# A scan's input term in a PSUM bank of its own, five shared banks in place of six, and a new order of the work

## The reference, cut to what matters

```python
def step(h, inp):
    dtt, ut, bt, ct = inp
    dA = dtt[:, :, None] * A
    barA = jnp.exp(dA)
    inp_term = jnp.einsum('bdn,bn,bd->bn', dA, bt, ut)
    h = barA * h + inp_term[:, None, :]
    y = jnp.einsum('bdn,bn->bd', h, ct) + Dp * ut
    return (h, y)
```

## Time and profile before

| | |
|---|---|
| median of 3 runs | 3253.51 us (3250.42 to 3253.90) |
| the profiled execution: time, span | 3258.51 us, 3256.8 us |
| busy in the span: PE, DVE, ACT, POOL | 78%, 76%, 58%, 35% |
| mean granted TensorE clock | 0.884 of full speed |
| DMA: packets' share of 16 engines | 34.3% |

### The profile page before, as it was taken

The page is one execution under the profiler, slowest core; times in us unless marked ns, Lnnn a source line. Parts: engine busy times, 40 slices in busy tenths (PEclk is TensorE's granted clock), DMA queues, the critical chain, the costliest instruction groups (busy, mean ns, idle before and its releaser), DMA issues.

```text
span 3256.8 us, 44290 instructions
## 1 busy us (share of the span) xinstructions
PE 2547.0 (78%) x12844; PEld 1449.3 (45%) x12908; DVE 2482.7 (76%) x4197; ACT 1884.0 (58%) x3613; POOL 1127.5 (35%) x1601
## 2 busy tenths in 40 slices
PE   3438788797879888797978879697887979787875
PEld 1104445353535445363544535354453535445553
DVE  6468787978778797878879797788868788776642
ACT  3356657574755657475655748466574746644331
POOL 2003243433434343333334333343333334333331
PEclk8569799898989899898989989899988989888896
DMA  2344433434343333434333343334334343331000
GB/s 61 68 72 60 53 50 46 62 42 66 38 60 49 51 53 46 63 40 64 44 50 51 46 66 39 60 44 54 52 42 66 39 65 43 53 43 26 4 4 7
DMA packets 95654, 157.96 MB, mean 49 GB/s; under 512 B 10722, under 2 KB 29358, under 8 KB 95406
## 3 DMA queue, kind: packets, MB, share of 16 engines
q1 hardware_dynamic: 95406, 154.96, 34.3%
HBM read 12.33 MB, written 8.39 MB: 6 GB/s over the span
## 4 chain that ended last, share of the span: by engine, by line
PE 32%; DVE 21%; ACT 18%; issue 10%; DMA 8%; SPq 6%; POOL 5%; DVEq 0%; ACTq 0%; POOLq 0%
DMA scan_bufs<-dt 7%; PE bank L938 6%; PE bank L921 6%; SPq L480 6%; DVE scan_bufs L1210 4%; ACT p_xT L647 4%; DVE rounding L1077 3%; PE bank L978 2%; PE acc_y L886 2%; PE bank L959 2%; PE bank L918 2%; POOL f_h L565 2%; ACT scan_bufs L637 2%; ACT masked_scores L688 2%; DVE f_h_max L1104 2%
## 5 line engine op out<-in xcount | busy, mean ns | idle before, releaser
L1210 DVE TENSOR_TENSOR_SCAN scan_bufs<-scan_bufs,inp 128x512 f32<-128x512 f32 x512 | 714.0, 1394 | 66.5 <-ACT scan_bufs L639 56.7
L637 ACT ACTIVATE scan_bufs<-scan_bufs,a_rows 128x512 f32<-128x512 f32 x512 | 366.4, 716 | 345.8 <-DMA scan_bufs<-dt 343.9
L921 PE MATMUL bank<-w_gu,f_xqT 128*128 128x512 f32 x1024 | 509.3, 643 | 30.2 <-ACT f_xqT L688 28.5
L886 PE MATMUL acc_y<-scan_bufs,sel_y 128*32 128x512 f32 x1024 | 308.8, 685 | 225.7 <-DVE scan_bufs L1220 225.2
L938 PE MATMUL bank<-w_dn,f_hqT 128*128 128x256 f32 (+1 forms) x1536 | 425.8, 424 | 34.1 <-issue 24.8
L565 POOL TENSOR_TENSOR f_h<-f_h,f_h_inv 128x704 f32<-128x704 f32 x128 | 222.9, 1742 | 484.4 <-DVE f_h_inv L1108 484.4
L938 PEld LDWEIGHTS bank<-w_dn,f_hqT 128*128 128x128 f32 (+1 forms) x1536 | 301.4, 209 | 172.8 <-issue 131.5
L1220 DVE TENSOR_TENSOR scan_bufs<-scan_bufs,c_bank 128x512 f32<-128x512 f32 x512 | 338.2, 661 | 8.1 <-DVE x L1238 1.7
L583 POOL TENSOR_SCALAR_AFFINE_SELECT masked_scores<-masked_scores 128x512 f32<-128x512 f32 x256 | 190.2, 767 | 436.1 <-ACT masked_scores L688 436.1
L639 ACT ACTIVATE scan_bufs<-scan_bufs 128x512 f32<-128x512 f32 x512 | 322.6, 630 | 16.2
L565 POOL TENSOR_TENSOR f_h<-f_h,f_h_scale 128x704 f32<-128x704 f32 x128 | 195.7, 1529 | 388.8 <-DVE f_h L1079 388.8
(11 more groups left out here) (192 smaller groups left out, 4710.4 us busy)
## 6 DMA issues: line engine op xcount, KB each, us to landing
scan_bufs<-dt SPq DMA_DIRECT2D x512, 256.0 KB
xp<-L_attn_a_x SPq DMA_DIRECT2D x16, 512.0 KB, 7.6
out<-x SPq DMA_DIRECT2D x64, 128.0 KB, 1.7
w_attn<-L_attn_b_W_attn SPq DMA_DIRECT2D x1, 768.0 KB
scan_bufs<-L_ffn_w_gate SPq DMA_DIRECT2D x1, 704.0 KB
scan_bufs<-L_ffn_w_up SPq DMA_DIRECT2D x1, 704.0 KB
masked_scores<-L_ffn_w_down SPq DMA_DIRECT2D x1, 704.0 KB
w_in<-L_attn_a_w_in SPq DMA_DIRECT2D x1, 256.0 KB, 2.8
```

What stands on the lines that cost most here:

```text
L637: nc.scalar.activation(half, half, ACT.Exp, scale=a_rows[:, c, at:at + 1]).then_inc(root_ready, 1)
L886: last = nc.tensor.matmul(acc_y[32 * j:32 * j + 32, :], sel_y[:, q, :], bar[n % SLOTS][:, h, :], start=(q == 0), stop=(q == 3), tile_posit ...
L921: last = nc.tensor.matmul(to[:, :], f.xqT[:, k, :], w_gu[:, k, g, lo:hi], start=(k == 0), stop=(k == DH - 1))
L1210: nc.vector.tensor_tensor_scan(half, half, inp[par][:, :], 0.0, ALU.mult, ALU.add)\
```

## The change

- `inp` becomes one PSUM bank (`inp_bank`); the pool falls from six banks to five, and `Banks` deals them out anew.
- ACT copies the B projection to a new SBUF tile `b_rep`, one for all batches, and waits first until the "inp" step of the batch before has read it.
- DVE's "inp" reads `b_rep` and G's bank and writes `inp_bank`; before that it waits for the last scan of the batch before. Its place moves over the border of the bodies: in the order of DVE the next body now begins with the two last residuals, then "inp", then scan 0.
- The scans read `inp_bank`.
- `TIMES` is set anew for all engines.

```diff
-        inp = [sb(f"inp{i}", [P, T]) for i in range(2)]
+        b_rep = sb("b_rep", [P, T])
...
-        acc_y, c_rep = bank("acc_y"), bank("c_bank")
-        banks = [bank(f"bank{j}") for j in range(6)]
+        acc_y, c_rep, inp = bank("acc_y"), bank("c_bank"), bank("inp_bank")
+        banks = [bank(f"bank{j}") for j in range(5)]
...
                 elif step == "B":
-                    evac(step, inp[par][:, :])
+                    if not first(b):
+                        wait_drained(act, "P", b - 1, 0, "G")
+                    evac(step, b_rep[:, :])
...
                     src, done = wait_filled(dve, "P", b, 0, "G")
-                    nc.vector.tensor_tensor(inp[par][:, :], inp[par][:, :], src[:, :], ALU.mult).then_inc(done, 1)
+                    if not first(b):
+                        dve.wait_ge(scans_done, upto(b - 1, HALVES, HALVES - 1))
+                    nc.vector.tensor_tensor(inp[:, :], b_rep[:, :], src[:, :], ALU.mult).then_inc(done, 1)
...
-                nc.vector.tensor_tensor_scan(half, half, inp[par][:, :], 0.0, ALU.mult, ALU.add)\
+                nc.vector.tensor_tensor_scan(half, half, inp[:, :], 0.0, ALU.mult, ALU.add)\
                     .then_inc(scans_done, 1)
```

More of the change, by code:

```diff
@@ L44 @@
     "sp": {
-        ("P", "load"): 2.8, ("G", "spread"): -1.75, ("R2", "down"): 12.8,
+        ("P", "load"): 1.9, ("G", "spread"): -2.1, ("R2", "down"): 13.8,
     },
     "pe": {
[1 row of a table removed]
[1 row of a table added]
         ("P", "B"): 16.5, ("P", "C"): 32.25, ("P", "dt0"): 20.5, ("P", "dt1"): 23.7, ("P", "G"): 29.6,
[2 rows of a table removed]
[2 rows of a table added]
         ("R1", "a_s0"): 16.2, ("R1", "a_s1"): 17.35, ("R1", "a_sum"): 18.1, ("R1", "a_flip"): 19.3,
[2 rows of a table removed]
[2 rows of a table added]
     },
     "act": {
[1 row of a table removed]
[1 row of a table added]
         ("P", "u0"): 11.4, ("P", "u1"): 14.2, ("P", "low"): 15.55, ("P", "B"): 17.9, ("P", "exp0"): 21.7,
[2 rows of a table removed]
[2 rows of a table added]
         ("R1", "a_turn"): 14.0, ("R1", "a_qkv"): 15.0, ("R1", "a_q"): 15.0, ("R1", "a_s0"): 16.0,
         ("R1", "a_s1"): 17.0, ("R1", "a_sum"): 18.0, ("R1", "a_turn_y"): 20.0, ("R2", "abs_x"): 3.2,
[1 row of a table removed]
[1 row of a table added]
     },
     "dve": {
[3 rows of a table removed]
[3 rows of a table added]
         ("R1", "down"): 11.2, ("R1", "a_qkv"): 15.1, ("R1", "a_sum"): 18.1, ("R1", "a_flip"): 19.25,
[2 rows of a table removed]
[2 rows of a table added]
     },
     "pool": {
[4 rows of a table removed]
[4 rows of a table added]
     },
```

## The result

The changed kernel takes 3239.23 us (median of 5 runs, 3236.76 to 3243.04), the kernel before 3253.51 in the same comparison: ratio 0.9963, 95% interval 0.995 to 0.9975. It is faster, by 12 us by the ratio and 14 by the medians, where 32.5 were forecast; the time lies within the range of my own case (3195 to 3247), on its slow side. The profiled execution took 3240.98 us, its span is 3239.1 (before 3258.51 and 3256.8).

A forecast was written before the change was run, and what follows sets the result against it. DVE was taken to pace the first stage, PE the second, a chain the third. Per body 1.8 + 2.5 + 1.6 - 1.9 - 1.5 = 2.5 us, times 13 is 32.5, from 3253.5 to 3221 us; range 3155 to 3285.

The forecast's parts named there:

- my own case: The prediction's main case, forecast 3221 us, own range 3195 to 3247, chance 0.38.
- 13 x 2.5: The sum: 13 bodies have all parts and gain 2.5 us each, 32.5 us in all.
- The scans are free and PSUM costs nothing: Scans no longer collide with POOL; with a PSUM operand they stay at 1.218 us, ends +-1.0 us in the first stage.
- First stage, 1.8 us: Stage paced by DVE: 16 scans fall from 21.32 to 19.5 us, gain 1.8 us a body.
- Second stage, scans nothing: Stage paced by PE: 9 scans stand 3.5 us above free ones, but relief there gains nothing.
- Third stage, 2.5 us: End of a body: masks directly behind "du" shorten PE's wait of 3.75 us to about 0.3; gain 2.5 us.
- Border, 1.9 us: "inp" and scan 0 (0.68 + 1.22 us) move behind DVE's wait for PE between bodies; cost 1.9 us.
- SP's queue, 1.6 us: Spread 2 ahead of the store removes most of DVE's 1.9 us load wait; gain 1.6 us, ends 0 and 2.6.
- Five banks, 1.5 us: Fewer PSUM banks make PE wait for earlier readers, mainly in the second stage; cost 1.5 us, ends 0 and 5.
- Rival C: Bank waits land in full where PE bounds: 6.2 us replace 1.5, -2.2 a body, 3282 us; chance 0.22.
- Other beats, 0: Remaining reordering, such as R2's norms and R1's statistics up to a beat earlier, counted at 0.
- Head and tail have no scans beside POOL work worth counting: Outside the 13 bodies with all parts, the change was counted as giving nothing.

The follow-up runs named there:

- e4: The changed kernel with inp in one SBUF tile in place of the PSUM bank, so scans have two SBUF inputs again: 3285.26 us, ratio 1.0096.
- e1: The changed kernel with the three beats of SP's queue as before (store ahead of spread 2): 3251.11 us, ratio 0.9993.
- e8: The kernel before with a pool of five banks in place of six and nothing else: 3349.15 us, ratio 1.0310.
- e7: The changed kernel with all of `TIMES` as before, "inp" at 31.5: 3278.18 us, ratio 1.0084.
- e6: The changed kernel with inp in one SBUF tile and a pool of six banks: 3264.27 us, ratio 1.0046.
- e3: The kernel before with its loop written out, so no jump back: 3232.64 us, ratio 0.9932.
- e2: The changed kernel with its loop written out, so no jump back: 3197.10 us, ratio 0.9822.
- e14: The kernel before with the three new beats of SP's queue and nothing else: 3240.56 us, ratio 0.9957.
- e13: The changed kernel with a loop of two turns of four bodies, one jump back in place of four: 3217.04 us, ratio 0.9888.
- e11: The changed kernel with its loop, inp and scan 0 on DVE ahead of the border again: 3219.73 us, ratio 0.9877.
- e5: The changed kernel with spread 2 behind the store only in the first body of each loop turn: 3277.72 us, ratio 1.0084.
- e15: The changed kernel with its loop, inp and scan 0 ahead of the border, and SP's three beats as before: 3220.74 us, ratio 0.9911.

## Why the prediction was right and wrong

The sign was right, and so was the mechanism of the relief; the size was not: 12 to 14 us for 32.5. The step that failed is the last of the sum, "13 x 2.5", which takes all bodies as alike. By the steps:

- **The scans are free and PSUM costs nothing: right.** The median is 1212 ns for 1218. The rule of the Trainium skill ("VectorE: DVE Perf Modes", the TRN2 errata), by which a PSUM source would have cost 65 ns a scan by estimate, is not borne out by the 512 scans; that a two-input operation with one input in PSUM contends with nothing (the Trainium skill, "SBUF — State Buffer", Who interferes with whom) is.
- **First stage, 1.8 us: too small.** e4 against the changed kernel gives 3.3 a body there. I priced DVE's side of a collision and not POOL's: the operand took 89 us off DVE's busy time and 192 off POOL's, and PE waits 141.1 us for POOL's scales (L565) in the changed kernel and 156.3 in e4. That this makes up the missing 1.5 us is argued, not shown.
- **Second stage, scans nothing: right** (e4: within 0.2).
- **Third stage, 2.5 us: right in size** (3.2), and it is mostly the beats that give it: with inp in SBUF the new order has 34.7 already, before 37.4. PE waited 53.7 us in all for masks (29 times) and now never does.
- **Border, 1.9 us: too small.** It is 2.2 with the loop and 3.1 without. I priced the two moved operations on DVE, but not that PE waits behind them for `u` (15.4 us in all before, 48.3 after). The wait of 2 us or more that I named as a sign is 1.35 ahead of the residual, for 0.48.
- **SP's queue, 1.6 us: a half.** On the old order it is 1.1, on the new 0.8, without jumps 0. The load wait that I priced is mostly gone under the new beats in either order: in e1 it is 4.3 us in all for 24.3.
- **Five banks, 1.5 us: right for the new beats (1.2), wrong for the beats I derived it from (5.7 in a plain body, 7.8 by the whole time).** I laid the new assignment on the times of before, counted a dozen early takes by 0.1 to 4 us, and put "a mean near 1.9" on the largest, which is 3.4 in e8. Rival C's mechanism is real there, and its 6.2 a body was near; that 1.5 came out right for the changed kernel is luck, since it was derived on the other order. What keeps it small is the step that I put at nothing:
- **"Other beats, 0": a step that failed.** On five banks the new beats (border and queue with them) gain 39 us (e7), on six they lose 15 (e6). In a plain body of six banks with inp in SBUF the second part is 63.4 us for 59.9, before the bank is taken: here lie 3.5 of the 4.6 us that the second part lost. Without jumps the same cuts give 85.3, 63.4 and 37.6 us for the kernel before (e3) and 84.5, 66.3 and 33.6 for the changed one (e2), so a part's length hangs on more than the work in it.
- **"13 x 2.5", all bodies alike: the step that failed most.** Four of the 13 end in a jump back; they were to gain 10 us and lost 18.3. That is 28 us between forecast and result. At a jump engines stand, and longer in the changed kernel (DVE 12.7 to 13.1 us for 3.0 to 4.2), and PE's next product runs at a granted clock of 0.50 to 0.52 for 0.59 to 0.63. Written out, without jumps, the change gives 36 us.
- **"Head and tail have no scans beside POOL work worth counting": wrong the other way**, by some 25 us. Body 16 has all 32 scans beside R1 and R2; it gained 10.4, of which 4.7 by the scans (e4). Body 17 gained 5.0 by the order of work (e4 and e6 have the same, e3 and e14 have the 152.9 us of before). The 4.9 of body 18 are not the change's: e3, which has the order of before, and e14, which differs from it on SP alone, take 96.3 us there for 103.8, and the mean granted clock of the stretch is 0.67 in the kernel before, 0.72 in e3 and 0.71 in the changed one.

Taken one at a time from the changed kernel's side, with the loop: scans +43, queue +10, bank -16, border -28, together 9 of the 12 us. With four differences, each uncertain by 6 to 9 us, and the other beats left out, that is a weak check. From the side of the kernel before, one step behind the other, the same 12 is made of bank -101, PSUM operand +74 and beats +39. This sum closes by its making; what it shows is that the worth of a part hangs on the order it stands in.

What stays open: why PE's standstill at the jump is 5.8 to 7.0 us with either queue (e13, with a turn of four bodies, has 9.2), how much the lower clock behind a jump costs beyond that one product, and which of the other beats lengthen the second part. The plain bodies between two with a jump are 3 to 6 us longer in e1 and e11 than those ahead of the loop; their mean granted clock is 0.90 for 0.92 in e1 and 0.89 for 0.925 in e11, with PE busy some 3 us more in e11, which goes with part of it.

## What to carry to other kernels

- Before multiplying a gain by the number of bodies, cut the trace at the same instruction in each body and look whether the bodies are alike: four of them were 6 to 7 us longer before the change too, and that was in the trace. A loop's jump back is a place where engines stand for 3 to 13 us here and PE starts again at a lower granted clock; if the code may be long, write the loop out (46 and 22 us here). Fewer transfers in flight at the jump shortened DVE's standstill (e1, e5, e15), but none of these kernels got faster by it.
- A collision between two engines costs on both (89 us of DVE and 192 of POOL here); price what waits behind each of them. A resource taken away (here a bank) is priced on the order it will be used in, not on the old one.
- When work is moved behind a wait, the wait shows its price in the next stage as well. Try the move alone: the fastest version here is the changed kernel without it, written out (3157 us, 3.0% under the kernel before).

## What the runs showed of the hardware

- A scan of 128x512 with one operand in PSUM takes 1158 to 1223 ns beside all POOL work of this kernel; with both in SBUF 1158 to 3265 ns (e4).
- Behind a jump back an engine stands idle for 3.0 us (ACT, DMA engines at 13% around it) to 12.25 us (DVE, DMA engines at 46%). The first q14 packet starts within 0.5 us of DVE's last operation in the first case and 8.4 to 9.8 us behind it in the second, with 256 KB transfers in flight.
- After PE stood 5.8 to 6.5 us at a jump, 12 matmuls of 128x256 take 4.79 to 5.79 us at a granted clock of 0.63 to 0.50, where they take 3.02 at 1.00.
